# q and the score weights of a conditioned attention layer: Wq and Wk as stationary tiles, cond and q moving

## What is computed

```python
# x (2, 2048, 512), cond (2, 512), every W (512, 512), 16 heads of 32
q = cond @ Wq.T + bq                       # one query row for each batch
k = x @ Wk.T + bk
v = x @ Wv.T + bv
scores = einsum('bhqd,bhkd->bhqk', q / sqrt(32), k)
attn = clip(scores, 0.0, 1.0)
out = x + (attn[..., None] * v) @ Wo.T + bo
```

## Time and profile before

| | us |
|---|---|
| median of three timed runs | 186.25 (186.05 to 186.3) |
| the profiled execution, its own time | 186.12 |
| span of its trace | 184.3 |
| PE busy | 180.6 |
| VectorE busy | 169.8 |
| ScalarE busy | 115.7 |
| GpSimd busy | 14.3 |

### The profile page before, as it was taken

One profiled execution on the slowest core, in us unless ns is written; L12 is line 12 of the kernel. 1 busy time (PEld: TensorE's weight loads), 2 busy tenths in 40 slices (PEclk: granted clock), 3 DMA queues, 4 the chain that ended last, 5 costly groups with the idle time before them and its releaser, 6 DMA issues.

```text
span 184.3 us, 2383 instructions
## 1 busy us (share of the span) xinstructions
PE 180.6 (98%) x803; PEld 147.7 (80%) x803; DVE 169.8 (92%) x186; ACT 115.7 (63%) x158; POOL 14.3 (8%) x20
## 2 busy tenths in 40 slices
PE   8999999999999999999999999999999999999993
PEld 2788888888878888888888888888888888888883
DVE  1999997998699999999999999999999999989963
ACT  3789873796587754765667764783486854766200
POOL 8000000000000020121000010111000001111000
PEclk9999999999999999999999999999999999999999
DMA  6999910027701017289568617399920207489786
GB/s 216 345 392 429 401 63 2 0 59 233 283 13 44 21 36 117 114 131 230 94 244 282 238 39 114 121 147 312 274 119 0 57 0 115 131 127 295 132 343 228
DMA packets 9355, 30.13 MB, mean 163 GB/s; under 512 B 1152, under 2 KB 1536, under 8 KB 9216
## 3 DMA queue, kind: packets, MB, share of 16 engines
q1 hardware_dynamic: 7616, 23.70, 35.6%
q0 software_dynamic: 1728, 6.29, 20.6%
HBM read 19.50 MB, written 8.39 MB: 151 GB/s over the span
## 4 chain that ended last, share of the span: by engine, by line
PE 98%; DVE 0%; issue 0%
PE bank_y L354 9%; PE bank_y L358 9%; PE bank_y L356 9%; PE bank_x L354 8%; PE bank_x L358 8%; PE bank_x L356 8%; PE bank_z L354 6%; PE bank_z L358 6%; PE bank_z L356 6%; PE bank_x L429 4%; PE score_bank L415 4%; PE score_bank L414 4%; PE bank_z L429 3%; PE bank_z L474 2%; PE bank_x L447 2%; PE bank_y L447 1%
## 5 line engine op out<-in xcount | busy, mean ns | idle before, releaser
L858 DVE TENSOR_TENSOR form_lo<-work,form_hi 128x1024 fp32r<-128x1024 f32 (+1 forms) x38 | 40.3, 1081 | 2.9 <-ACT form_hi L579 2.6
L579 ACT CAST form_hi<-work 128x1024 fp32r<-128x1024 f32 x28 | 29.1, 1051 | 20.7 <-PE score_bank L415 6.9
L614 ACT ACTIVATE work<-bank_y,const 128x512 f32<-128x512 f32 x30 | 19.7, 686 | 9.2 <-PE bank_y L358 9.2
L841 POOL DMA_DIRECT2D work<-x_t x12 | 10.5, 875 | 154.8 <-DVE work L891 148.0
L354 PE MATMUL bank_x<-form_hi,wo_hi 128*128 128x512 f32 x52 | 20.3, 391 | 0.0
L358 PE MATMUL bank_x<-form_hi,wo_lo 128*128 128x512 f32 x52 | 20.2, 389 | 0.0
L356 PE MATMUL bank_x<-form_lo,wo_hi 128*128 128x512 f32 x52 | 20.2, 389 | 0.0
L614 ACT ACTIVATE work<-bank_x,const 128x512 f32<-128x512 f32 x24 | 15.9, 685 | 6.4 <-PE bank_x L358 5.8
L880 DVE SCALAR_TENSOR_TENSOR work<-relu,work 128x1024 f32<-128x1024 f32 x16 | 19.4, 1220 | 0.3 <-ACT relu L643 0.3
L354 PE MATMUL bank_y<-form_hi,wv_hi 128*128 128x512 f32 x48 | 18.7, 389 | 0.0
L356 PE MATMUL bank_y<-form_lo,wv_hi 128*128 128x512 f32 x48 | 18.7, 389 | 0.0
(11 more groups left out here) (150 smaller groups left out, 389.8 us busy)
## 6 DMA issues: line engine op xcount, KB each, us to landing
x_raw<-x_t SPq DMA_DIRECT2D x16, 512.0 KB, 6.3
out_t<-work SPq DMA_DIRECT2D x14, 512.0 KB, 3.6
work<-x_t POOLq DMA_DIRECT2D x12, 512.0 KB, 5.9
score_others<-score_rows SPq DMA_DIRECT2D x16, 128.0 KB, 2.3
work<-first_t SPq DMA_DIRECT2D x2, 512.0 KB, 3.7
work<-wq_t SPq DMA_DIRECT2D x2, 512.0 KB, 8.0
work<-wk_t SPq DMA_DIRECT2D x2, 512.0 KB, 11.0
work<-wo_t SPq DMA_DIRECT2D x1, 1024.0 KB, 13.4
```

What stands on the lines that cost most here:

```text
L579: nc.scalar.copy(flat(form_hi, kind), raw(kind, phase)).then_inc(hi_ready[kind], 1)
L614: nc.scalar.activation(result_set(phase)[:, q, j * ROWS:(j + 1) * ROWS], of[:, j, :], ACT.Identity, bias=bias[:, tile:tile + 1], scale=sca ...
L841: pool.dma_start(output_set(s)[:, q, :], x_t[s, q], accum_op=ALU.add).then_inc(residual_added[q], 16)
L858: return nc.vector.tensor_tensor(to, of, hi.bitcast(F32), ALU.subtract)
```

## The change

`rows` becomes `columns`. The 128x128 tiles of Wq's and Wk's parts are now the stationary operands, and the parts of cond (4 columns: hi and lo of two batches) or of q (64 columns: hi and lo of 32) move. There are 4 output tiles by 4 input tiles by 2 parts of the weight, 32 matmuls for q and 32 for a. The result comes out with features on partitions, so the copies of the rows and the turning matmuls go; instead VectorE adds the hi column and the lo column (one more small addition in `scale_q`, one in `fill_a`). The zeros in the places of cond and q go too, with the two constants. `columns` waits for the hi and the lo parts before it starts. On PE the product of W21 with T3 now stands ahead of the score weights' matmuls as it did ahead of the turning, so that the job for a is in one piece between it and W22's product. ScalarE's and VectorE's lists are rearranged around it.

```diff
+            def columns(out, parts, hi_semaphore, lo_semaphore):
+
                 pe.wait_ge(hi_semaphore, KT)
-                for k in range(KT):
-                    pe.matmul(out[:, :], vectors[:, k, :], qk_tile(form_hi, k), start=k == 0, stop=False)
                 pe.wait_ge(lo_semaphore, KT)
-                for k in range(KT):
-                    mm = pe.matmul(out[:, :], vectors[:, k, :], qk_tile(form_lo, k), start=False, stop=k == KT - 1)
+                for m in range(MT):
+                    for k in range(KT):
+                        for of in (form_hi, form_lo):
+                            mm = pe.matmul(out[:, m, :, :], qk_tile(of, k)[:, m * P:(m + 1) * P], parts[:, k, :, :],
+                                           start=k == 0 and of is form_hi, stop=k == KT - 1 and of is form_lo)
                 return mm
...
             pe.wait_ge(cond_ready, 1)
-            rows(q_rows_psum, cond_parts, wq_hi_ready, wq_lo_ready).then_inc(q_rows_done, 1)
+            columns(q_psum, cond_parts, wq_hi_ready, wq_lo_ready).then_inc(q_done, 1)
 
             first_product(banks[2], W11, T3, True, False)
-
-            pe.wait_ge(q_rows_ready, 1)
-            for m in range(MT):
-                mm = pe.matmul(q_psum[:, m, :], q_rows[:, m * P:(m + 1) * P], const[:, C_PAIR:C_PAIR + BATCH],
-                               start=True, stop=True)
-            mm.then_inc(q_done, 1)
-
             first_product(banks[2], W12, B22, False, True)
-
-            pe.wait_ge(q_parts_ready, 1)
-            rows(a_rows_psum, q_parts, wk_hi_ready, wk_lo_ready).then_inc(a_rows_done, 1)
 
             pe.wait_ge(first_out[Q11], 2)
             first_product(banks[0], W21, T3, True, False).then_inc(w21_done, 1)
 
             pe.wait_ge(q_ready, 2)
             pe.matmul(c_psum, const[:, C_SAME:C_SAME + P], bk_q[:, :, :], start=True, stop=True)
-            pe.wait_ge(a_rows_ready, 1)
-            for k in range(KT):
-                mm = pe.matmul(a_psum[:, k, :], a_rows[:, k * P:(k + 1) * P], const[:, C_FOLD:C_FOLD + BATCH * HEADS],
-                               start=True, stop=True)
-            mm.then_inc(a_done, 1)
+            pe.wait_ge(q_parts_ready, 1)
+            columns(a_psum, q_parts, wk_hi_ready, wk_lo_ready).then_inc(a_done, 1)
...
                 if phase == 1 and kind in (T1, T2):
 
-                    act.wait_ge(a_rows_done, 1)
+                    act.wait_ge(a_done, 1)
...
             def wk_part(m):
 
                 act.wait_ge(wk_loaded[m // 2], 16)
-                act.wait_ge(q_rows_done, 1)
+                act.wait_ge(q_done, 1)
...
             wk_part(0)
-            copy_q_rows()
             wk_part(1)
...
             hi(T1, 1)
-            copy_a_rows()
             wo_sum_part(S2, 1)
             wv_sum_part(S3, 3)
             hi(T2, 1)
+            hi(B11, 1)
+            first_values(Q22, banks[0], 6)
             wo_sum_part(S3, 2)
-            first_values(Q22, banks[0], 6)
-            hi(B11, 1)
             hi(B21, 1)
...
-            nc.gpsimd.memset(cond_home.bitcast(F32), 0.0).then_inc(zeros_ready, 1)
-            nc.gpsimd.memset(q_home.bitcast(F32), 0.0).then_inc(zeros_ready, 1)
...
                 dve.wait_ge(q_sum_ready, 1)
+                nc.vector.tensor_tensor(q_sum[:, :, :], q_sum[:, :, :], q_psum[:, :, 1, :], ALU.add).then_inc(q_sum_ready, 1)
+                dve.wait_ge(q_sum_ready, 2)
...
                 dve.wait_ge(a_full_ready, 1)
+                nc.vector.tensor_tensor(a_full[:, 0:KT, :], a_full[:, 0:KT, :], a_psum[:, :, 1, :], ALU.add).then_inc(a_full_ready, 1)
+                dve.wait_ge(a_full_ready, 2)
...
             scale_q()
+            scale_bk()
             x_t1(1)
-            scale_bk()
             x_t3(1)
             wo_part(W11, 0)
             wo_part(W12, 1)
             wo_sum(1)
-            lo(T1, 1)
+            wo_sum(2)
             fill_a()
             split_a(0)
+            lo(T1, 1)
             x_t2(1)
             sum_c()
-            wo_sum(2)
             wv_sum_part(S3, 3)
             lo(T2, 1)
+            lo(B11, 1)
             x_t4(1)
             wo_sum_part(S2, 1)
-            lo(B11, 1)
             lo(B21, 1)
```

More of the change, by code:

```diff
@@ L31 @@
 C_HEAD = C_SAME + P
-C_FOLD = C_HEAD + HEADS
-C_PAIR = C_FOLD + BATCH * HEADS
-C_COND = C_PAIR + BATCH
+C_COND = C_HEAD + HEADS
 C_COLS = C_COND + KT * BATCH
@@ L173, in build @@
         cond_hi_ready, cond_ready = sem("cond_hi_ready"), sem("cond_ready")
-        q_rows_done, q_rows_ready, q_done = sem("q_rows_done"), sem("q_rows_ready"), sem("q_done")
+        q_done = sem("q_done")
         q_hi_ready, q_parts_ready = sem("q_hi_ready"), sem("q_parts_ready")
-        a_rows_done, a_rows_ready = sem("a_rows_done"), sem("a_rows_ready")
         q_sum_ready, q_ready = sem("q_sum_ready"), sem("q_ready")
@@ L682, in wq_part @@
                 nc.scalar.copy(qk_tile(form_hi, k), wq_raw(k)).then_inc(wq_hi_ready, 1)
-            def copy_q_rows():
-                act.wait_ge(q_rows_done, 1)
-                nc.scalar.copy(q_rows, q_rows_psum[:, :]).then_inc(q_rows_ready, 1)
-            def copy_a_rows():
-                act.wait_ge(a_rows_done, 1)
-                nc.scalar.copy(a_rows, a_rows_psum[:, :]).then_inc(a_rows_ready, 1)
             def wk_part(m):
                 act.wait_ge(wk_loaded[m // 2], 16)
-                act.wait_ge(q_rows_done, 1)
+                act.wait_ge(q_done, 1)
                 nc.scalar.copy(qk_tile(form_hi, m), wk_raw(m)).then_inc(wk_hi_ready, 1)
@@ L1030, in wk_part @@
             def wk_part(m):
-                dve.wait_ge(q_rows_done, 1)
+                dve.wait_ge(q_done, 1)
                 dve.wait_ge(wk_hi_ready, m + 1)
@@ L1042, in wo_sum_part @@
                 if form == S4:
-                    dve.wait_ge(a_rows_done, 1)
+                    dve.wait_ge(a_done, 1)
                 lo_part(flat(wo_lo, form), wblock(wo_sums, n), flat(wo_hi, form)).then_inc(wo_lo_ready[form], 1)
@@ L1064, in scale_q @@
                 dve.wait_ge(q_ready, 1)
-                nc.vector.tensor_copy(q_parts[:, :, 0:BATCH * HEADS], q_heads[:, :, :]).then_inc(q_hi_ready, 1)
+                nc.vector.tensor_copy(q_parts[:, :, 0, :], q_heads[:, :, :]).then_inc(q_hi_ready, 1)
                 dve.wait_ge(q_hi_ready, 1)
-                lo_part(q_parts[:, :, BATCH * HEADS:2 * BATCH * HEADS], q_heads[:, :, :],
-                        q_parts[:, :, 0:BATCH * HEADS]).then_inc(q_parts_ready, 1)
+                lo_part(q_parts[:, :, 1, :], q_heads[:, :, :], q_parts[:, :, 0, :]).then_inc(q_parts_ready, 1)
             def scale_bk():
-                dve.wait_ge(q_sum_ready, 1)
+                dve.wait_ge(q_sum_ready, 2)
                 nc.vector.scalar_tensor_tensor(
@@ L1312, in constant_columns @@
     const[:, C_HEAD:C_HEAD + HEADS] = head[:, None] == np.arange(HEADS)[None, :]
-    for first in (0, BATCH * HEADS):
-        const[first:first + BATCH * HEADS, C_FOLD:C_FOLD + BATCH * HEADS] = np.eye(BATCH * HEADS)
-    for first in (0, BATCH):
-        const[first:first + BATCH, C_PAIR:C_PAIR + BATCH] = np.eye(BATCH)
     const[:, C_COND:C_COLS] = cond.reshape(BATCH, KT, P).transpose(2, 1, 0).reshape(P, KT * BATCH)
```

24 lines of the change are left out of this document (10 added, 14 removed).

## The result

The change makes the kernel slower: 190.75 us (188.81 to 191.46, four executions) against 186.28 us (186.05 to 186.32), ratio 1.0234 with a 95% interval from 1.0207 to 1.0262. The forecast was 188.0 us and its range ended at 190.0. The small matmuls cost what was said. What was given a chance of 0.14 came about: PE's clock falls at the end of q's run of them, and stays down for longer than priced.

A forecast was written before the change was run, and what follows sets the result against it. PE was taken as the bound, busy 180.6 of 184.3 us. Adding 7.43 us and removing 5.70 gave +1.73 on 186.12, 187.85 us; the timed median's 0.13 made 188.0 us, range 187.4 to 190.0.

The forecast's parts named there:

- third rival: On PE behind q's matmuls: clock falls, 4 us of work at half speed, +2.0 us, 190.0 us; chance 0.14.
- the sum: PE's opening: 7.43 us of new small matmuls against 5.70 us removed, +1.73 us.
- The price of the pairs: On PE, q's and a's 64 loads with their matmuls: 0.1114 us each, at most 0.120 us.
- The rule on fast weight loads: PE's loads: non-FP32 weights load at about twice the speed; if fp32r counts, the 64 pairs cost half.
- the first rival: PE's fp32r loads are cheap: half of 0.1114 us a pair, -1.84 us, 184.4 us; chance 0.07.
- Wq's lo parts: Wait ahead of q's matmuls on PE: parts end 1.7 us before they are needed, cost nothing.
- W21's product: Moved ahead of a's matmuls on PE: q's parts then come in time, cover 1.9 us, cost nothing.
- Score weights: VectorE's work ahead of `scores(0, 0)`: done at 34.12 us, needed at 34.80, cover 0.45 us after the load.
- 0 to 0.3: Cover in us between ScalarE's `copy_b11(1)` and PE's `product_t2(1)`; no cost taken, up to 0.3 us for the range.
- the fourth rival: New wait at `product_t2(1)` or `scores(0, 0)`: a further 1 us slip costs 0.5 to 1 us; chance 0.12.

The follow-up runs named there:

- e7: Kernel before the change, with the four fp32 matmuls that turn q done four times over (32 records instead of 8): 191.78 us, ratio 1.0283.
- e9: Changed kernel with q's and a's matmuls each moving 128 columns, both runs unbroken: 188.11 us, ratio 1.0122.
- e11: Changed kernel measured once more without any edit: 191.11 us, ratio 1.0291.
- e8: Against e5: first half of a's matmuls put ahead of W21's product, c and the second half behind its first group: 190.89 us, ratio 1.0298.
- e2: Changed kernel with q made by rows and turned as before the change, a by columns: 188.53 us, ratio 1.0150.
- e5: Changed kernel with q's small matmuls in four pieces of 8 and a's in two of 16, between large matmuls: 188.95 us, ratio 1.0146.
- e1: Changed kernel with q's 32 matmuls moving 64 columns instead of 4: 190.87 us, ratio 1.0273.
- e3: Changed kernel with a made by rows and turned as before the change, q by columns of 4: 188.82 us, ratio 1.0168.

## Why the prediction was wrong, point by point

**The step that failed** is the third rival, "PE's clock falls during the small matmuls": its chance of 0.14, its place outside the sum, and its price. Against it I had put that "0.9 us of such matmuls at 20.98 leave the next product at full speed". That is true and says nothing of four times the length: e7 turns those same matmuls four times over, and the clock falls in every execution. For the price I took a stretch of 4 us at half, +2.0 us; it was 6.8 us in both traces of the changed kernel, +3.2 us, and the mean clock of seven of its eight executions says the same. "190.0 us for one fall" thus should have been 191.2. The rival was named, with the sign and the mechanism right, and it should have been the likeliest case.

**The price of the pairs** was right. 0.1114 us from the earlier trace rows came back as 0.112 us in the trace after and in e9; fp32r loads cost what fp32 loads cost, and the number of moving columns, 4 to 128, doesn't count. The whole opening with the clock up is +1.69 us against +1.73 (e9).

**The rule on fast weight loads** (the Trainium skill, TensorE: Matmul & The Clock Gate, section Weight-path perf modes), by which the change would have gained: the first rival is out. The trace does not agree with a fast load for fp32r; a pair stayed at 0.111 to 0.112 us.

**The covers.** Wq's lo parts: hidden, but with less to spare than the forecast's 1.7 us: the last of them ended 0.64 us ahead of q's first matmul in the first trace of the changed kernel (15.49 and 16.13 us) and 1.27 us ahead in e11 (14.58 and 15.85). W21's product: e8 measured 1.57 us of waiting without it, in the kernel with the pieces. Score weights: VectorE and ScalarE in the changed kernel, against the earlier trace rows, in two pieces of their timelines:

```profile
35.03 0.29 DVE L1052 COPY a_full<-score_bank 128x128 f32<-128x128 f32 x1 [4.62 <-PE score_bank L454]
35.36 0.29 DVE L1054 TENSOR_TENSOR a_full<-a_full,score_bank 128x128 f32<-128x128 f32 x1
...
36.48 0.55 DVE L832 TENSOR_TENSOR a_for_hi<-a_full,a_for_hi 128x384 fp32r<-128x384 f32 x1
```

```profile
39.34 1.06 ACT L565 CAST form_hi<-x_sum 128x1024 fp32r<-128x1024 f32 x1 [2.16 <-DVE x_sum L930]
...
47.68 1.27 ACT L600 ACTIVATE work<-bank_y,const 128x512 f32<-128x512 f32 x2
```

The weights are done at 36.48 + 0.55 = 37.03 us, the scores start at 37.68: 0.65 us, less 0.2 for the load, is the 0.45 of the forecast. `copy_b11(1)` ends at 48.95 us and `product_t2(1)` starts at 49.47, its load 0.2 us before: 0.3 us, the upper end of "0 to 0.3". (The "1.5 us" given there for before leaves out the load, which the new figure counts; with it that cover was 1.3 us.) Neither became a wait, so the fourth rival did not happen.

**What stays open.** With the clock up the changed kernel's work (e9) is 2.3 us above before (ratio 1.0122), 0.5 us more than the sum. In the profiled executions the opening explains +1.69 us and the end behind the last matmul +0.46 (185.8 - 182.12 against 3.22); the beginning, 0.66 us earlier in that execution (the clock rose sooner, as above), goes the other way. Why the last stores land 3.2 to 3.5 us behind the last matmul in some kernels and 3.7 to 4.7 in others was not found. Also open are e2's two executions with an extra 1.3 us and no fall on record. Nothing between 64 and 128 columns was tried, nor pieces between 2.0 us and the whole run; and it is open why the same kernel falls in one execution and not in another.

## What to carry to other kernels

A long run of small matmuls costs its loads, about 0.111 us each, and can cost the clock as well: here 3.6 us of them brought 3.4 or 6.8 us at half speed in most executions, which is worth 1.7 to 3.3 us, as much as or more than the 1.7 us that the 64 matmuls add by themselves. If such a run can't be avoided, let the matmuls move more columns than are needed: up to 128 for each load were free in time, and 13 executions kept their clock. Or break it up with large matmuls: pieces of up to 2.0 us kept it in e5's four executions, but there is little to spare, since the clock fell after 2.2 us of a run in e7, and behind a wait and a piece of 1.8 us in e8. Turning a product so that the big matrix is stationary gains nothing when each of its tiles is used for a few columns only; eight matmuls of 512 columns and a turning of 0.9 us beat 32 loads, 2.75 against 3.6 us.

## What the runs showed of the hardware beside this

- The distance between loads follows PE's clock: pairs with 4 columns stood 0.112 us apart at 2.4 GHz and 0.21 us apart at 1.2 GHz in the changed kernel. PE's busy time is 2.00 of 2.00 us in the windows of both.
- An fp32r matmul of 128 columns is hidden under its load: 32 pairs took 3.52 us (15.79 to 19.31) in e9, 0.110 us each, as with 4 or 64 columns (0.112 us) and as fp32 records with 2 columns (0.111 us).
- The falls lasted for 3.4 or 6.8 us in the traces. The mean granted clock of an execution gives their sum without a trace (0.991 for 3.4 us, 0.982 for 6.8), but not their number: e1's profiled execution has 0.982 from two falls of 3.4 us, 14 us apart. The two executions of e2 at 1.00 whose 1.3 us are unexplained show no fall at all.
- A fall began 2.2 us (e7), 2.7 us (e11) and 3.0 us (the changed kernel) behind the first record of the run, and in e3 4.8 us behind it, when the run was over.
